# Kept rows and column marks of the self-attention stage: from VectorE to GpSimd

## The reference, cut to what matters

```python
def _L0_attn_ref(inputs, W, proj, concat_w, concat_b):      # inputs = layernorm(x)
    hp = jnp.tanh(jnp.einsum('sbh,hk->sbk', inputs, W))
    scores = jnp.einsum('sbk,k->sb', hp, proj)
    mask = t_idx[None, :] < t_idx[:, None]
    logits = jnp.where(mask[:, :, None], scores[None, :, :], neg)
    attn = jax.nn.softmax(logits, axis=1)
    context = jnp.einsum('tsb,sbh->tbh', attn, inputs)
    cat = jnp.concatenate([inputs, context], axis=-1)
    out = jnp.tanh(jnp.einsum('tbc,hc->tbh', cat, concat_w) + concat_b)
    out = out.at[:2].set(inputs[:2])
    return out

x = x + _L0_xattn_ref(_layernorm(x), ...)
x = x + _L0_attn_ref(_layernorm(x), ...)
x = x + _L0_ffn_ref(_layernorm(x), ...)     # top 2 of 8 experts by a gate
```

## Time and profile before

| | us |
|---|---|
| median of 3 runs | 594.68 |
| the three runs | 593.76, 594.68, 599.95 |
| profiled execution, its own time | 597.04 |
| its span, first to last instruction | 595.2 |
| PE busy | 580.7 (98%) |
| DVE busy | 460.2 (77%) |
| ACT busy | 351.3 (59%) |
| POOL busy | 329.7 (55%) |

### The profile page before, as it was taken

The page is one execution under the profiler, slowest core; times in us unless marked ns, Lnnn a source line. Parts: engine busy times, 40 slices in busy tenths (PEclk is TensorE's granted clock), DMA queues, the critical chain, the costliest instruction groups (busy, mean ns, idle before and its releaser), DMA issues.

```text
span 595.2 us, 21920 instructions
## 1 busy us (share of the span) xinstructions
PE 580.7 (98%) x8431; PEld 480.3 (81%) x8431; DVE 460.2 (77%) x1064; ACT 351.3 (59%) x769; POOL 329.7 (55%) x481
## 2 busy tenths in 40 slices
PE   8999999999999999999999999999899999999997
PEld 3888878888788888788888788888478888887596
DVE  4688867878678887777777686698878888888485
ACT  3677868878677777677767344645443333332463
POOL 3457867787758787578886232012266666653000
PEclk9999999999999999999999999999799999999999
DMA  8725553775545746585520199445633334342894
GB/s 230 185 68 121 143 190 101 226 180 192 164 134 168 203 160 202 176 229 182 170 83 4 38 430 401 164 148 197 205 115 133 133 133 134 133 134 91 296 344 119
DMA packets 65398, 102.13 MB, mean 172 GB/s; under 512 B 15280, under 2 KB 41968, under 8 KB 64400
## 3 DMA queue, kind: packets, MB, share of 16 engines
q1 hardware_dynamic: 59440, 84.59, 44.7%
q0 software_dynamic: 4992, 15.34, 7.7%
q10 hardware_dynamic: 864, 0.79, 0.5%
HBM read 69.43 MB, written 31.27 MB: 169 GB/s over the span
## 4 chain that ended last, share of the span: by engine, by line
PE 55%; POOL 20%; issue 14%; DVE 6%; DMA 3%; ACT 1%; POOLq 0%; SPq 0%; DVEq 0%
PE bank L2013 12%; PE scores L2013 6%; PE bank L1058 5%; PE bank L1065 5%; PE bank L1090 4%; POOL hA L732 4%; POOL lA L728 4%; PE bank L2041 4%; POOL hA L724 4%; PE scores L1106 3%; PE scores L1079 3%; PE scores L1242 2%; POOL Mb L765 2%; POOL tm L756 2%; PE scores L1995 1%
## 5 line engine op out<-in xcount | busy, mean ns | idle before, releaser
L864 DVE TENSOR_SCALAR Pm<-scores 128x514 f32<-128x514 f32 x128 | 88.1, 688 | 53.4 <-PE scores L1079 52.5
L980 ACT ACTIVATE Pm<-Pm,nm 128x257 f32<-128x257 f32 x256 | 115.7, 505 | 2.5 <-DVE nm L869 2.5
L869 DVE TENSOR_REDUCE nm<-Pm 128x2 f32<-128x514 f32 x128 | 87.5, 684 | 2.2
L975 ACT ACTIVATE PT<-bank 128x512 f32<-128x512 f32 x64 | 38.3, 598 | 75.3 <-PE bank L1090 75.3
L1058 PE MATMUL bank<-hA,wH 128*128 128x258 f32 x256 | 75.2, 304 | 0.3 <-POOL hA L732 0.3
L1090 PE MATMUL bank<-cst,Pm 128*128 128x128 f32 x512 | 69.9, 279 | 0.0
L1058 PE MATMUL bank<-hA,wL 128*128 128x258 f32 x256 | 69.2, 281 | 0.0
L1065 PE MATMUL bank<-wH,hA 128*128 128x256 f32 x256 | 68.9, 281 | 0.0
L1065 PE MATMUL bank<-wL,hA 128*128 128x256 f32 x256 | 68.8, 280 | 0.0
L2013 PE MATMUL bank<-W,xh 128*128 x208 | 67.0, 403 | 0.5 <-ACT xh L1943 0.5
L765 POOL TENSOR_TENSOR Mb<-Os,rc 128x64 f32<-128x64 f32 x64 | 21.8, 340 | 74.7 <-DVE rc L889 74.3
(11 more groups left out here) (299 smaller groups left out, 1460.1 us busy)
## 6 DMA issues: line engine op xcount, KB each, us to landing
w_d<-whl SPq DMA_DIRECT2D x64, 256.0 KB, 3.5
W<-w_d SPq DMA_DIRECT2D x6, 2048.0 KB, 17.8
wst<-in_W1T SPq DMA_DIRECT2D x32, 256.0 KB, 3.6
cg<-g_d SPq DMA_DIRECT2D x16, 512.0 KB, 5.3
cx<-in_ctxT SPq DMA_DIRECT2D x31, 258.0 KB, 3.0
cx<-in_ctxT SPq DMA_DIRECT2D x62, 129.0 KB, 3.5
bb<-in_b SPq DMA_DIRECT2D x8, 512.0 KB, 6.4
W<-w_d SPq DMA_DIRECT2D x5, 512.0 KB, 5.2
```

The lines of the kernel that those rows point to most:

```text
L864: v.tensor_scalar(Pm[:, i % 2, 2 * p:2 * p + 2, :], S4[:, 2 * p:2 * p + 2, 0:NK], -CLAMP, CLAMP, ALU.max, ALU.min).then_inc(s_cl, 1)
L869: v.tensor_reduce(nm[:, i % 2, 2 * p:2 * p + 2], Pm[:, i % 2, 2 * p:2 * p + 2, :], AX.X, ALU.max, negate=True).then_inc(s_nm, 1)
L975: a.activation(PT[:, i % 2, 0, :, :].rearrange("p a b -> p (a b)"), held("p", i, 0)[:, :], ACT.Copy).then_inc(s_pte[0], 1)
L980: a.activation(Pm[:, i % 2, g, :], Pm[:, i % 2, g, :], ACT.Exp, bias=nm[:, i % 2, g:g + 1]).then_inc(s_ex, 1)
```

## The change: what it does

DVE's `kept` goes, and so do its four comparisons of 128x512 in `marks` for chunks 0 and 1. POOL gets both, in another form:

- `kept(c)` no longer adds `xn`. For a kept row, x + (x * rs + nb) is x * (1 + rs) + nb, so POOL makes two columns of factors, `kf` (m10 * rs + 1, and m10 * nb), and then one operation for each of the four tiles: xb = xb * factor + factor, 128x256, with one pair of factors per row. ACT's norm of the next chunk and SP's load of a bias no longer wait for it, since it doesn't read `xn`.
- `columns(c)` for c = 0 and 1 compares `i16` with one rest per row, in eight operations of 128x128. PE's `slots` waits for them by `u_as`, in halves. Later counts of `u_as` are moved up by four.

```diff
@@ slots
                 t.wait_ge(u_ab, 2 * c + k + 1)
                 if (c, k) in ((2, 0), (3, 1)):
-                    t.wait_ge(u_as, c - 1)
+                    t.wait_ge(u_as, c + 3)
+                if c < 2:
+                    t.wait_ge(u_as, 2 * c + k + 1)
@@ marks
-                mine = c < 2 or (c == 3) != (k == 1)
+                mine = c >= 2 and (c == 3) != (k == 1)
@@ SP
                 sp.wait_ge(u_t, 8)
-                sp.wait_ge(u_b2, 4)
                 load_bias(1)
@@ DVE
-                def kept(c):
-                    if c == 0:
-                        v.wait_ge(u_xv, 2)
-                    v.wait_ge(u_xn, on_scalar(c))
-                    v.scalar_tensor_tensor(out=xb[:, 4 * c:4 * c + 4, :], in0=xn[:, :, :], scalar=m10,
-                                           in1=xb[:, 4 * c:4 * c + 4, :], op0=ALU.mult, op1=ALU.add).then_inc(u_b2, 1)
@@ third
-                    v.wait_ge(u_b2, c + 1)
+                    v.wait_ge(u_b2, 6 * c + 6)
@@ POOL
+                def kept(c):
+                    k = slice(4 * c, 4 * c + 4)
+                    if c >= 2:
+                        g.wait_ge(u_b2, 6 * (c - 1))
+                    g.tensor_scalar(kf[:, c % 2, 0, :], rs[:, k], m10, 1.0, ALU.mult, ALU.add).then_inc(u_b2, 1)
+                    g.tensor_scalar(kf[:, c % 2, 1, :], nb[:, 0, k], m10, 1.0, ALU.mult, ALU.mult).then_inc(u_b2, 1)
+                    g.wait_ge(u_b2, 6 * c + 2)
+                    if c == 0:
+                        g.wait_ge(u_xv, 2)
+                    g.wait_ge(u_xn, on_scalar(c))
+                    for j in range(4):
+                        n = 4 * c + j
+                        g.tensor_scalar(xb[:, n, :], xb[:, n, :], kf[:, c % 2, 0, j:j + 1], kf[:, c % 2, 1, j:j + 1],
+                                        ALU.mult, ALU.add).then_inc(u_b2, 1)
+
+                def columns(c):
+                    g.wait_ge(u_rf, c + 1)
+                    if c == 0:
+                        g.wait_ge(u_i16, 3)
+                    else:
+                        g.wait_ge(u_iv, c)
+                    for j in range(8):
+                        ins = g.tensor_scalar(A16[:, j, :], i16[:, :], rf[:, c % 2, 0, j // 4, j % 4:j % 4 + 1], 1.0,
+                                              ALU.is_equal, ALU.mult)
+                        if j % 4 == 3:
+                            ins.then_inc(u_as, 1)
@@ POOL, the loop
                     if 0 <= k - 2 < 4:
                         scales(1, k - 2, f_mv, f_r, f_rs)
+                    if k < 4:
+                        kept(k)
+                    if 0 <= k - 3 < 2:
+                        columns(k - 3)
                     if k + 2 < 4:
                         scales(0, k + 2, u_mv, u_r, u_rs)
@@ ACT, normed
                         a.wait_ge(u_t, 2 * c)
-                        a.wait_ge(u_b2, c)
```

More of the change, by code:

```diff
@@ L294, in build @@
         pf = put("pf", [128, 2, NTILE])
+        kf = put("kf", [128, 2, 2, 4])
         area(167, 199)
@@ L1423, in _ @@
                 t.wait_ge(r_sel, 1)
-                t.wait_ge(u_as, 3)
+                t.wait_ge(u_as, 7)
                 t.matmul(b[:, 0:40], iT[:, :], sel[:, :], start=True, stop=True).then_inc(r_i, 1)
@@ L1602, in _ @@
                         masked(k - 1)
-                    if k < 4:
-                        kept(k)
                     if k == 5:
```

## The result

| | before | after |
|---|---|---|
| median, us (5 runs each) | 594.81 | 600.26 |
| lowest to highest | 593.76 to 599.95 | 598.37 to 601.69 |
| profiled execution, its own time | 597.04 | 598.37 |
| span | 595.2 | 596.2 |

The changed kernel is **0.7% slower**: ratio 1.0073, 95% interval 1.0038 to 1.0109. That is some 4.3 us (2.3 to 6.5), and the median of 600.26 lies outside the range on record, 593.0 to 598.0. The ratio of the two medians in the table is 1.0092, inside the same interval. The time before in the table has two runs more than the one the prediction started from.

The account below looks back on a forecast made before the run. The prediction took PE to bound the stage, so of 7.2 us off DVE at most 0.35 counts; between -0.35 and 0.0 for engines blocking each other it took -0.2: 594.68 - 0.2 = 594.5 us, range 593.0 to 598.0.

Parts of the forecast that it names:

- What bounds the stage: From 382 to 412 us PE, busy 29.85 of 30.00 us, is the bound, though the chain of waits runs through DVE.
- The most that could be gained: PE ends slots(1) at 412.28 and starts the last chunk's turning at 412.63: at most 0.35 of DVE's 7.2 us.
- DVE is the bound after all: Rival: all DVE work removed after 382 us, 3.6 us, is gained, giving 591.1 us; chance 4%.
- Kept rows: On POOL, 0.41 us per operation, 2.0 us for a chunk, hidden by POOL's idle time, so they cost nothing.
- the 0.25 of the forecast: In round 3, DVE's reciprocal at 391.31 waits for ACT's last exponential, so DVE gains 0.25 of 1.20 us there.
- The price of a mark: One column mark of 128 columns on POOL: 0.30 us, eight 2.4 us, in time for PE's slots in both rounds.
- The bound at the other end, 1.02: A power of 4 columns on POOL takes 1.02 us; kept as the upper price of an operation, for the range.
- Both points from which the prediction let it decide: Marks cost nothing up to 0.64 us each in round 3; in round 4 they decide from 0.30 to 0.49 us.
- POOL's marks are dear, and PE waits for them: Rival, slower: at 0.6 us each 595.6 to 597.1, at 1.02 601 us; chances 24% (0.35 to 0.95 us) and 6% (dearer).
- The two engines in each other's way: POOL's marks and DVE's three operations exclude each other; at worst, all in a row, round 4's gain falls to 0.0.
- The Trainium skill's price for branching code: About 12 cycles a column on POOL, 1.28 us a mark, some +10 us, 605; chance 3 in 100.
- The clock: Rival: the half-speed stretch from 417 to 424 us shifts, 1 us either way, 593.5 to 595.5; chance 6%.

Follow-up runs that it names:

- kept rows alone: Changed kernel with DVE making all column marks again and only the kept rows left on POOL; ratio 1.0007 to the kernel before.
- a quarter of the marks: Changed kernel with POOL making only the second half of chunk 0's column marks, DVE the others, kept rows on POOL; ratio 1.0007 to the kernel before.
- half of them: Changed kernel with POOL making only the second halves of chunk 0's and 1's column marks, DVE the first, kept rows on POOL; ratio 0.9989 to the kernel before.
- chunk 1 alone: Changed kernel with POOL making the column marks of chunk 1 only, DVE those of chunk 0, kept rows on POOL; ratio 1.0104 to the kernel before.
- multiplications to spare: Changed kernel, but DVE makes all marks; POOL does eight multiplications per chunk into an unread buffer, and PE waits for them; ratio 1.0067 to the kernel before.
- marks alone: Changed kernel with the kept rows back on DVE in their old form and the column marks left on POOL; ratio 1.0077 to the kernel before.
- first wait filled: Changed kernel with two unused PE matmuls of 128x512 between the halves of slots(0), where PE waited 2.07 us; ratio 1.0088 to the kernel before.

## Why the prediction was wrong

**What bounds the stage: right.** PE was the bound and the chain through DVE misled: 4.8 to 6.0 of the 7.2 us off DVE were worth nothing that a measurement shows (kept rows alone 1.0007, a quarter of the marks 1.0007 with the turning 0.10 earlier, half of them 0.9989); all 7.2 without waits of PE was not run. The most that could be gained, 0.35 us, can't be told apart from that. That DVE is the bound after all fell with it: by that rival a quarter of the marks, 1.8 us of DVE's time behind 382 us, would give 0.997, and the interval is 0.9993 to 1.0022.

**Kept rows: right in effect, the size off.** 0.55 us each instead of 0.41, all in POOL's idle time. What I had not priced is that they hold DVE. Its attention weights of round 3 took 1.44 us (above), beside the last two of the kept rows' operations; before they took 0.87:

```profile
391.51 0.87 DVE L1512 TENSOR_TENSOR Ab<-L,sm 64x256 f32<-64x256 f32 x2
```

The earlier trace rows shows the pattern. The reciprocal ahead of them did come 0.22 us earlier into the stage, about the 0.25 of the forecast, but T16 starts 0.4 us later (57.39 us into the stage against 57.02) and not earlier; with the kept rows back on DVE and the marks on POOL it starts at 57.02. It moved no measured time.

**The price of a mark: the step that failed.** "I take 0.30": worked out from a multiplication by constants and right for that to the hundredth. A comparison with a scalar per row takes 0.71, so the term 8 x 0.30 = 2.4 us for a chunk's marks was 6.56 and 6.39 us with DVE's share. The bound at the other end, 1.02, held it. I chose the near end by the shape of the instruction (one tensor, two constants, so many columns), while what sets the price is its operator; and the same rows had the hint, a power at five times a multiplication. Both points from which the prediction let it decide were passed: 0.64 for round 3, and 0.30 to 0.49 for round 4.

**The rival was the outcome.** "POOL's marks are dear, and PE waits for them", with its own sum at 0.71 instead of 0.6. Round 3: 394.77 + 1.49 + 5.68 - 399.88 = 2.06 us late; the wait was 2.07. By the way it went at 1.02, the logits come at 401.2 + 2.06 = 403.26, DVE's rests 0.99 later at 409.25, and 409.33 + 1.49 + 5.68 + 0.41 = 416.9 against 412.63: 4.3. The turning came 4.21 later. That both fit so well is luck: two errors cancel. POOL began at 57.45 us into the stage and not at 56.85, since DVE's rests came later, and its eight marks took 6.56 us and not 1.49 + 5.68 = 7.17. In round 4 it began at 72.15 and not at 71.41, and they took 6.39. The mechanism is the rival's, its sum to within some 0.7 us a term. Its time by that, 594.68 + 4.3 = 599.0, is inside what was measured (594.81 x 1.0038 to 1.0109 is 597.1 to 601.3). It had 24 in 100, and the range left out its upper part, above 598.0.

**The two engines in each other's way: right for the marks.** All eight marks and DVE's three operations one behind the other was the worst case. With comparisons some of DVE's time fell between them: 6.56 - 5.68 = 0.88 of 1.49 us in round 3, 0.71 in round 4. With chunk 1 alone it was 1.35, but there DVE's sums of the last chunk fell into the run as well. The multiplications to spare show the effect more strongly: 1.3 us for an operation of 0.37, beside two of DVE's in a row. This is the rule of the Trainium skill, SBUF — State Buffer, section "Who interferes with whom", and the rows agree with it; those of 16 bits do so too.

**The Trainium skill's price for branching code** (GPSIMD Engine Reference, section "Elementwise — side-by-side cycle accounting"), 1.28 us by the estimate in the prediction, was too high: 3.3 ns for a column and 0.29 us fixed is what the rows show. Its direction was right where my choice from the rows was wrong.

**The clock.** I allowed it 1 us by itself, but it moved with PE's waits. Ahead of the turning a fall of 3.3 us put DVE's rests some 0.5 us later, which the turning did not show. Behind it the rest was 1.0 to 1.4 us longer than the kernel before's 14.44 in the five executions with 10.2 us or more at half clock; the changed kernel's own profiled execution, with 6.9, is not one of them.

## What to carry to other kernels

A price from a row holds for its operator: before work goes to GpSimd, find a row with the same operator there, or time one operation, since a comparison costs four times as much for a column as a multiplication. A handover is free as long as the slowest plausible price fits into the time between its input and its use (here 3.9 us for eight operations), and picking the near one of two bounds is no answer when the far one doesn't fit. And where a chain of waits runs through a busy engine beside a PE that is full, taking work off that engine buys nothing, while an input that keeps PE waiting is paid for. Waits in two rounds need not add up, though: the first can use up part of the second.

## What the hardware showed that I had not expected

- POOL's comparison of one tensor: 0.72 us for 128 columns, 2.00 for 512, whether f32 or f16 goes in or out; multiplication 0.37 and 0.69 with a scalar per row, 0.30 and 0.62 with constants.
- DVE holds POOL in 16 bits as well: two operations of 128x512 with two f16 tensors each, 0.74 and 0.68 us in a row, made a POOL multiplication of 0.37 us take 1.31. Beside DVE's marks of one f16 tensor it took 0.38.
- The stretch at half clock behind the turning is not one of fixed length: 6.8 or 6.9 us in most of the profiled executions, 10.2 or 10.3 in four, 13.7 in the one with waits of PE of 2.04 and 2.38 us within one round. The length of the last wait alone does not decide it: behind 2.51 us (marks alone) it was 6.8, behind 2.50 (first wait filled) 10.2. What does stays open.
- Behind a wait of PE of some 2 us in round 4 the clock fell in two of six profiled executions (2.07 and 2.09 us) and not in four (1.77, 2.02, 2.05 and 2.45). When it falls there and when not stays open too.
